# Three new sets of waits on GpSimd's indirect DMAs in a four-layer graph network kernel

## The reference, cut to what matters

```python
edge_index = jnp.stack([src, dst])
# layer 0, three times: m = h @ weight[i]
agg = jax.ops.segment_sum(m[src], dst, num_segments=n_nodes)
h = gru_cell(agg, h, w_ih, w_hh, b_ih, b_hh)
...
# layer 1, hypergraph: the same edges once forward, once back
e_feat = B_inv[:, None] * jax.ops.segment_sum(h[row], col, num_segments=num_edges)
out = D_inv[:, None] * jax.ops.segment_sum(e_feat[col], row, num_segments=num_nodes)
...
# layer 2, attention over the edges of a source
ee = jnp.exp(leaky_relu(s1[src] + s2[dst]) - emax[src])
out = jax.ops.segment_sum(attn[:, None] * mapped[dst], src, num_segments=N)
...
# layer 3, a small network on each edge
e_in = jnp.concatenate([x[src], x[dst]], axis=-1)
edge_new = _mlp(e_in, We1, be1, We2, be2)
agg = jax.ops.segment_sum(edge_new, dst, num_segments=x.shape[0])
```

## Time and profile before

| what | us |
|---|---|
| median of 3 runs | 4749.77 (4746.3 to 4755.25) |
| span of the profiled execution | 7303.0 |
| span less median | 2553 |
| POOL busy in that span | 2658.9, with 2706 instructions |
| PE busy in that span | 4076.2 |

### The profile page before, as it was taken

How to read it: one execution, slowest core, us unless ns; L and a number is a source line. 1 busy time by engine, 2 the same in 40 slices (tenths; PEclk the granted TensorE clock), 3 DMA queues, 4 the chain that set the end, 5 groups by cost and what they waited for, 6 DMA issues and landing times. The chain is left out here.

```text
span 7303.0 us, 82736 instructions
## 1 busy us (share of the span) xinstructions
PE 4076.2 (56%) x24237; PEld 3354.5 (46%) x24238; DVE 3381.7 (46%) x7886; ACT 2340.3 (32%) x3120; POOL 2658.9 (36%) x2706
## 2 busy tenths in 40 slices
PE   4332641019981111117989798988672197666655
PEld 2111420007761101106778586858571197665644
DVE  4222540358970000106788776456451076555545
ACT  0000010005640000004555455557461075444433
POOL 4555157730017777770000000000427601444463
PEclk7665865559995555558999898989785598888777
DMA  9400000009970000116658287843444343444432
GB/s 376 155 0 0 0 2 0 0 23 334 368 250 0 0 0 0 28 25 222 232 189 293 96 293 214 296 162 95 132 125 124 97 139 98 132 132 130 130 95 67
DMA packets 364823, 923.20 MB, mean 126 GB/s; under 512 B 114026, under 2 KB 138716, under 8 KB 364531
## 3 DMA queue, kind: packets, MB, share of 16 engines
q1 hardware_dynamic: 214722, 650.09, 26.9%
q10 hardware_dynamic: 58609, 180.13, 6.4%
q0 software_dynamic: 91200, 89.42, 5.2%
HBM read 705.69 MB, written 213.71 MB: 126 GB/s over the span
## 5 line engine op out<-in xcount | busy, mean ns | idle before, releaser
L1741 POOL DMA_INDIRECT edges_halves<-local,gather_idx x832 | 854.9, 1027 | 791.7 <-SPq L372 505.4
L1680 POOL DMA_INDIRECT adj_t<-cell_val,cell_at x832 | 828.6, 996 | 465.2 <-issue 369.9
L862 PE MATMUL ps<-tiles_r,stage_r 128*128 128x512 f32 x2028 | 811.6, 400 | 158.2 <-issue 132.0
L1134 POOL DMA_INDIRECT big<-table,gather_idx x576 | 548.4, 952 | 832.3 <-DVE stage L1284 376.3
L869 PE MATMUL ps<-stage,big 128*128 128x130 f32 x4046 | 520.1, 284 | 370.3 <-issue 354.7
L1134 POOL DMA_INDIRECT x_fm<-table,gather_idx x384 | 370.2, 964 | 959.8 <-DMA table<-cell_at 689.7
L869 PEld LDWEIGHTS ps<-stage,big 128*128 128x128 f32 x4046 | 497.9, 199 | 388.5 <-issue 384.6
L2059 PE MATMUL ps<-big,ident_h 128*128 128x104 bf16 (+1 forms) x2880 | 359.7, 256 | 460.4 <-issue 459.7
L1253 PE MATMUL ps<-big,stage 128*128 x1920 | 356.2, 342 | 352.7 <-issue 189.3
L1319 PE MATMUL ps<-ident,big 128*128 128x128 f32 x260 | 73.3, 377 | 817.2 <-issue 768.2
L2442 DVE TENSOR_TENSOR big<-ps,stage 128x1248 bf16<-128x1248 f32 x192 | 270.7, 1451 | 519.5 <-remote 385.1
(11 more groups left out here) (482 smaller groups left out, 9007.8 us busy)
## 6 DMA issues: line engine op xcount, KB each, us to landing
onehot<-adj_t SPq DMA_DIRECT2D x332, 512.0 KB
big<-adj_t SPq DMA_DIRECT2D x332, 512.0 KB
onehot<-adj_s SPq DMA_DIRECT2D x170, 512.0 KB
adj_t<-rows ACTq DMA_DIRECT2D x13, 6656.0 KB
adj_s<-big ACTq DMA_DIRECT2D x157, 512.0 KB, 5.3
stage<-local_rows SPq DMA_DIRECT2D x120, 512.0 KB
big<-adj_s SPq DMA_DIRECT2D x84, 512.0 KB
x_fm<-adj_s SPq DMA_DIRECT2D x84, 512.0 KB
```

What stands on the lines that cost most here:

```text
L862: nc.tensor.matmul(psum_fm(p, n)[:, 0:cut], upper_rows[:, k, :], tile[:, 0:cut], start=k == 0, stop=False, skip_group_check=True)
L1134: return nc.gpsimd.indirect_dma_start(out, None, table[0:N, :], bass.IndirectOffsetOnAxis(gather_idx[:, t:t + 1], 0))
L1680: nc.gpsimd.indirect_dma_start(out, bass.IndirectOffsetOnAxis(cells[:, c:c + 1], 0), cell_val[:, c:c + 1], None).then_inc(S(name), 16)
L1741: nc.gpsimd.indirect_dma_start(edges_halves, bass.IndirectOffsetOnAxis(slot_at[:, at:at + 1], 0), slot_val[:, at:at + 1], None).then_inc(h ...
```

## The change

Waits are added to POOL's program, nothing else: no instruction of another engine differs, and the indirect DMAs keep their order.

```diff
+TRIES_AHEAD, CELLS_TOGETHER = 11 / 20, 8
+EARLY_FROM, EARLY_TURNS = 50, 5 / 2
+SORTED_TOGETHER = 3
...
                 for u in range(2 * CH):
+                    if u % CH == 0:
+                        used = EARLY_FROM + math.floor(EARLY_TURNS * (2 * k + u // CH))
+                        pool.wait_ge(S("tile_used"), turns_before(len(MODES) - 1) + min(used, PASS_TURNS))
...
                 for c in range(UNITS[n]):
+                    if n < KEPT and (unit_from(n) + c) % CELLS_TOGETHER == 0:
+                        tries = TRIES + math.floor(TRIES_AHEAD * (unit_from(n) + c))
+                        pool.wait_ge(S("same_used"), min(tries, TRIES * SL))
...
                     nc.gpsimd.indirect_dma_start(edges_halves, bass.IndirectOffsetOnAxis(slot_at[:, at:at + 1], 0),
                                                  slot_val[:, at:at + 1], None).then_inc(halves_written[n % 2].sem, 16)
+                    if (c + 1) % SORTED_TOGETHER == 0:
+                        wait(pool, halves_written[n % 2], 16 * (SLW * (n // 2) + c + 1))
```

## The result

The changed kernel takes 5206.15 us (median of 4 runs, 5200.72 to 5214.17), the kernel before, run beside it, 4750.75 us: a ratio of 1.0964, 95% interval 1.0949 to 1.0980. It is 455 us slower. The forecast was 4735 us, the range 4640 to 4900.

A forecast was written before the change was run, and what follows sets the result against it. Bounds by stage: preparation by comparisons and counts, first pass by DMA, passes 1 to 4 and attention by PE, edge stage by PE, DVE and POOL in turns. 4750 + 0 + 0 + 0 - 15 = 4735 us, range 4640 to 4900.

The forecast's parts named there:

- stop of the traced kind: Other engines nearly stopping beside POOL's indirect-DMA bursts; claimed absent untraced, POOL's issue costing 0 to about 285 us.
- The rebuild from clean rates: Timed run summed by stages: 3735 us without the edge stage, leaving 1015 us for it.
- POOL's spacing: Time per POOL indirect DMA: 1.27 us traced, between 0.97 and 1.27 untraced, 1.12 taken.
- Part 1: Count matrix scatters paced by comparisons: 25 us lost at u = 8, hidden by the first pass; bounds 0 and +25, taken 0.
- Part 2: Sorted edges in threes, 272 waits: middle need 1367 us inside room 1307 to 1397, hidden before pass 4; taken 0.
- late by 428: High end for the sorted edges: scatters at 1.27 us, waits 1.7 us quiet and 3.35 loaded, late in pass 4.
- Part 3: Early gathers, eight per 2.5 attention turns from turn 50: no brake, hidden before ScalarE asks; 0, at most +10 us.
- Gains: Relief of other engines from thinned POOL bursts: at most 57% of 0 to 285 us, 0 to 162; taken 15.
- Rival (c): Larger relief from thinned POOL bursts, half of 162 us: -80, 4670 us; chance 0.14.
- The forecast of the trace: Profiled span near 6000 us instead of 7303, since thinned bursts stop the other engines less.
- (a): Pair rows come late in pass 4 through the sorted edges' landing waits: +110, 4860 us; chance 0.29.
- (b): First pass waits for the delayed count matrix if POOL needs 1.27 us: +25, 4775 us; chance 0.09.

The follow-up runs named there:

- the second trace: The kernel before, unchanged, profiled once more: measured 4748.18 us, profiled span 4746.4 us.
- the disturbed execution: First profiled execution of the kernel before, on which the prediction stood: span 7303 us, against a timed median of 4749.77 us.
- the run with the early gathers' waits alone: Kernel before plus only the waits tying the early gathers to the attention's used turns: 4746.22 us, ratio 1.0004.
- threes alone: Kernel before plus only a landing wait after every three sorted-edge scatters: 5175.39 us, ratio 1.0919.
- changed, eights: Changed kernel with a wait after every eight sorted edges instead of three: 4869.81 us, ratio 1.0265.
- changed, threes one group behind: Changed kernel, but after each three sorted edges GpSimd waits for the three before them, on two alternating semaphores: 4775.50 us, ratio 1.0072.
- changed, without the threes: Changed kernel without its wait for every three sorted edges, the other waits kept: 4773.31 us, ratio 1.0063.
- pacing of the matrix alone: Kernel before plus only the count matrix's scatter paced by the used comparisons: 4765.34 us, ratio 1.0044.
- changed, both steps mended: Changed kernel with the count matrix paced only from scatter 224 on and sorted edges in seventeens, early gathers as changed: 4748.37 us, ratio 1.0012.
- thirteens alone: Kernel before plus only a wait after every thirteen sorted edges: 4745.97 us, ratio 1.0002.
- pacing from 224 on: Kernel before plus only the count matrix's pacing by used comparisons, starting at scatter 224: 4744.88 us, ratio 1.0006.
- seventeens alone: Kernel before plus only a wait after every seventeen sorted edges: 4741.06 us, ratio 0.9996.

## Why the prediction was wrong

**What bounds the kernel.** Half right. That the timed run has no stop of the traced kind is confirmed by the second trace. The rebuild from clean rates was too short where it mattered. Two rows of the second trace of the kernel before, the first pass and the edge stage:

```profile
L646 PE MATMUL ps<-tiles_r,stage_r x508: 392/396/797, 693.8 to 1215.9; 128*128 128x512 f32 x170
...
L1253 PE MATMUL ps<-big,stage x1920: 274/275/578, 3810.9 to 4678.0; 128*128 x192
```

The edge stage takes 867 us and not the 1015 that I had left over for it. The other 148 are largely in the first pass (it ends at 1216, reckoned 1177) and the node update behind it, in passes 1 and 2 (330 us each, reckoned 317) and between the attention and the edge stage (3685.1 to 3810.9, 126 us, reckoned 73). That sum could be closed only by giving all that was unknown to one stage, and the agreement of 1015 with the traced 1036 looked like a proof; it was none, since the 1036 came from the disturbed execution.

**POOL's spacing, 1.12 us as the middle of 0.97 and 1.27.** Wrong. The 0.97 bound rested on the 0.30 gap being a cost of tracing. At a span equal to the timed run the gap is still 0.30 and a plain step 1.27. The two lines of scatters, first the count matrix, then the sorted edges:

```profile
L1680 POOL DMA_INDIRECT adj_t<-cell_val,cell_at x832: 964/971/1888, 86.6 to 1170.2; - x167
its engine sat idle before it (us, times) until:
  issue: 320.7, 832
...
L1741 POOL DMA_INDIRECT edges_halves<-local,gather_idx x832: 964/971/1494, 1228.6 to 2333.5; - x167
```

From first to last start the count matrix takes 1083.6 us, 1.30 a scatter with the changes of slab, and the sorted edges 1104.9 us, 1.33 a scatter beside the passes. The first trace had shown 1.27 for a plain step too; I had no row for anything less.

**Part 1: right mechanism, wrong value.** The 25 us at u = 8 were 26.4. The text said what happens at 1.27: "already late by 21, and 25 are added whole". Measured: PE stands 21.7 us between 1000 and 1100, and 22 are added. That 21 and 22 agree is partly luck: the text had the lateness at the last column group, from 1140 on, and the trace has most of it at a group before, with the load that SP issues at 1064; SP's second wait, 33.4 less 25.8 = 7.6 us, is the later one. Having taken 1.12, I booked 0. The term was +22.

**Part 2: the step that failed.** The mechanism was right, the need was not: 1367 us were taken as the middle, and 1775 were used. The room was right: from the first scatter at 1252.4 to DVE's request at 2595.3 (3039.8 less 444.5) are 1343 us, 1331 less the 12 for the pair gathers, inside 1307 to 1397. The need is 1331 + 444 = 1775. Of the 408 us that the middle lacked, two terms account for all. The scatters alone need 1106 us (1104.9 and the last one), not 832 x 1.12 = 932: 174 us. The waits add 1775 - 1106 = 669, 2.46 us each as the mean of 272, not 272 x 1.6 = 435: 234 us. Above a plain step a wait costs 3.85 us beside loads, where 3.35 was the upper end, and 1.17 in the quiet, where 1.5 to 1.7 were taken. The middle value had not been weighted by where POOL is: 1.6 us for all 272 waits, when 945 of 1307 us of the room lie beside loads at a DMA share of 0.86. Either error alone is enough to be late: 932 + 669 = 1601 and 1106 + 435 = 1541, both over 1397.

The end "late by 428" had both right in kind, took 1.7 and 3.35, and came within 17 us of the 444.5 measured, in part by luck, since its quiet wait was too long and its loaded one too short. The value between the ends was chosen by an untraced spacing for which no row spoke, and the load, for which rows did speak, was used only for the bound.

The Trainium skill ("DMA: Bandwidth & Descriptors", section "Anatomy of one DMA — SWDGE (gpsimd) path") states a fixed cost of about 2.0 us; the estimate from it, a need of 1171 us with no part late, would have led further off. Measured, the instruction and its wait take 0.97 + 1.47 = 2.4 us quiet, near that figure, and 0.97 + 4.15 = 5.1 beside loads, over twice as much.

**Part 3: right result, wrong reason.** 0 was forecast, 3 within error measured. But the gathers were not hidden. The first row is ScalarE's in the x3 stage of the second trace of the kernel before, the second the same in the run with the early gathers' waits alone; then the first gather and the attention's products of each:

```profile
  DMA early_rows<-x_fm: 77.1, 1
...
  DMA early_rows<-x_fm: 84.4, 1
...
3236.76 0.98 POOL L1134 DMA_INDIRECT x_fm<-table,gather_idx  x1 [686.38 <-DMA table<-cell_at]
L869 PE MATMUL ps<-stage,big x4046: 275/275/585, 3054.9 to 3685.1; 128*128 128x130 f32 x193
...
3240.80 0.95 POOL L1137 DMA_INDIRECT x_fm<-table,gather_idx  x1 [698.28 <-PE ps L872]
L872 PE MATMUL ps<-stage,big x4046: 275/275/587, 3048.7 to 3680.2; 128*128 128x130 f32 x193
```

In the kernel before the gathers start when the third table row group is stored, 182 us into the attention (3236.8 less 3054.9), and 384 of them with 24 stores take some 545 us, so they end 77 us after ScalarE asks. Their own pace of 1.42 us a gather (545/384) is slower than the turns they were tied to (3.70 x 2.5/8 = 1.16), so the tie does not brake them once they run. But it holds the first one: turn 50 is done 192 us into the attention (3240.8 less 3048.7), 10 us after the rows are there. In the six traces with the tie the first gather comes 191 to 192 us into the attention and ScalarE waits 78.2 to 84.4 us; in the six without it (the disturbed one left out) 182 us and 74.4 to 77.1. So some 77 us are in both kernels, and the tie adds about 7 to ScalarE's wait, which the timing of the part alone (-2 to +7 us) can neither show nor exclude.

**Gains: 15 us.** The right size (13 by the medians of threes alone), from the wrong source. Threes alone make passes 1 and 2 shorter by about 20 us together (first to last issue 320.6 and 319.6 against 329.4 and 330.5). Pass 1 with threes alone, and in the second trace of the kernel before:

```profile
L865 PEld LDWEIGHTS ps<-tiles_r,stage_r x508: 186/188/331, 1320.0 to 1640.6; 128*128 128x128 f32 x170
```

```profile
L862 PEld LDWEIGHTS ps<-tiles_r,stage_r x508: 186/188/333, 1325.3 to 1654.7; 128*128 128x128 f32 x170
```

The forecast's share of 57% counts 304 scatters of part 1, which no row gives; 624 are paced. Rival (c), a large relief, did not come: the 285 us it drew on were the 1015 us less 732, and with the measured 867 the same subtraction leaves 135.

**The forecast of the trace**, about 6000 us because thinned bursts would stop the others less: right in direction, for a reason that is refuted. The trace fell to 5207 with the change and to 4746 without any.

**Rivals and chances.** (a) happened, beyond its high end of 428, and (b) with it. Each had its condition written down. That of (b) was a spacing of 1.27; and at the measured spacing (a) too comes true from (1397 - 1106)/272 = 1.07 us a wait on, below both waits of the earlier trace rows. They were given chances as if they were separate, 0.29 and 0.09, and 1.27 as if it were the unlikely end. The range to 4900 cut off the bound that the text itself had worked out, 4750 + 428.

**All runs**, in short:

| kernel | us | ratio to before |
|---|---|---|
| changed | 5206.2 | 1.0964 |
| threes alone | 5175.4 | 1.0919 |
| changed, eights | 4869.8 | 1.0265 |
| changed, threes one group behind | 4775.5 | 1.0072 |
| changed, without the threes | 4773.3 | 1.0063 |
| pacing of the matrix alone | 4765.3 | 1.0044 |
| changed, both steps mended | 4748.4 | 1.0012 |
| before, the run with the second trace | 4748.2 | one run |
| early gathers alone | 4746.2 | 1.0004 |
| thirteens alone | 4746.0 | 1.0002 |
| pacing from 224 on | 4744.9 | 1.0006 |
| seventeens alone | 4741.1 | 0.9996 |

## What to carry to other kernels

A wait for the landing of what was just issued costs the rest of its flight each time (here 1.2 to 3.9 us); the same wait one group later costs almost nothing (4775 us against 4773 without it). Reckon such a wait by the load on the DMA engines where the instructions will be issued, and multiply by the number of waits before comparing with the room. If a traced span is far from the timed one, have the kernel profiled again before an argument is built on it, and do not close a sum by leaving the unknown to one stage.

## What the runs showed of the hardware

I had not expected that the wait for an indirect scatter's landing nearly triples, from 1.47 to 4.15 us, beside a load stream with a DMA share of 0.88, which leaves 12% of the DMA engines' time free; that the wait is the same after 3, 8 and 13 scatters (4.08, 3.92 and 4.12 us in pass 1); or that thinning 226 scatters in 300 us to 118 gives PE only 3% more matmuls (1235 to 1273). That the load causes the longer landing is read from stretches of one trace with and without it; no run here took the loads away.
